# LayerNorm of the attention input applied to transposed tokens, without TensorE transpositions

## The reference

```python
def _layernorm(x, axis=-1, eps=1e-05):
    m = jnp.mean(x, axis=axis, keepdims=True)
    v = jnp.var(x, axis=axis, keepdims=True)
    return (x - m) / jnp.sqrt(v + eps)

# attention: 16 heads of 64, 128 queries and 128 keys in each of 64 sequences
q, k, v = norm_x @ w_q, context @ w_k, context @ w_v
out = softmax(q k^T * 64 ** -0.5) v @ w_o + b_o
# feed-forward: 8 experts of width 512, the best 2 of softmax(x @ gate) weigh their outputs
h = relu(x @ W1[e] + b1[e]);  y = sum over the best 2 of gate_topk[e] * (h @ W2[e] + b2[e])
# block
x = x + attention(_layernorm(x), ctx_768)
x = x + feed_forward(_layernorm(x))
```

## Time and profile before

| what | us |
|---|---|
| median of 3 runs | 1580.39 (1580.01 to 1581.38) |
| profiled execution, its own time | 1580.22 |
| span of the profiled execution | 1578.5 |
| start until the steady iterations | 0 to about 58 |
| one iteration in steady state | 34.16 |
| expert phase | from about 1110 |

### The profile page before, as it was taken

How to read it: one execution, slowest core, us unless ns; L and a number is a source line. 1 busy time by engine, 2 the same in 40 slices (tenths; PEclk the granted TensorE clock), 3 DMA queues, 4 the chain that set the end, 5 groups by cost and what they waited for, 6 DMA issues and landing times.

```text
span 1578.5 us, 45424 instructions
## 1 busy us (share of the span) xinstructions
PE 1553.8 (98%) x14150; PEld 1454.0 (92%) x14151; DVE 1176.1 (75%) x3796; ACT 1108.0 (70%) x3357; POOL 818.1 (52%) x946
## 2 busy tenths in 40 slices
PE   8999999999999999999999999999999999999997
PEld 7899999999899999999999989998899999999997
DVE  4777777777777777777777777777788777777775
ACT  5677677677776777767767777676666676777774
POOL 2344545545554554554555455455456555555556
PEclk9999999999999999999999999999999999999999
DMA  6522111222111221211122211122799755555554
GB/s 201 145 72 74 60 60 60 77 90 72 62 60 60 67 94 66 74 60 60 63 75 89 74 60 60 60 67 81 241 231 249 144 86 85 89 86 90 84 84 61
DMA packets 105643, 145.05 MB, mean 92 GB/s; under 512 B 12736, under 2 KB 87616, under 8 KB 105344
## 3 DMA queue, kind: packets, MB, share of 16 engines
q1 hardware_dynamic: 60144, 89.00, 17.8%
q0 software_dynamic: 26816, 37.32, 13.7%
q10 hardware_dynamic: 18640, 18.19, 4.4%
HBM read 77.09 MB, written 67.38 MB: 92 GB/s over the span
## 4 chain that ended last, share of the span: by engine, by line
issue 47%; POOL 22%; PE 9%; DVE 7%; DMA 6%; DVEq 3%; ACT 2%; POOLq 2%; ACTq 1%; SPq 0%
POOL lists L662 7%; DMA out<-stage_room,number 6%; PE bank_a L1404 4%; POOL prob L669 3%; DVE hid L1332 3%; POOL rstd L648 2%; DVE stage_room L1349 2%; POOL stage_room L711 2%; POOL stage_room L707 2%; POOL out L735 2%; DVEq L1344 1%; PE bank_v L1437 1%; POOLq L729 1%; PE bank_s L1422 1%; DVEq L1323 1%
## 5 line engine op out<-in xcount | busy, mean ns | idle before, releaser
L669 POOL TENSOR_TENSOR prob<-prob,inv 128x512 f32<-128x512 f32 x256 | 271.4, 1060 | 520.3 <-DVE inv L956 519.6
L777 ACT ACTIVATE prob<-bank_s,low 128x128 f32<-128x128 f32 x1024 | 363.3, 376 | 40.9 <-DVE low L951 40.9
L735 POOL DMA_INDIRECT out<-stage_room,number x142 | 231.8, 1632 | 53.9 <-issue 53.1
L951 DVE TENSOR_REDUCE low<-bank_s 128x4 f32<-128x512 f32 x256 | 175.4, 685 | 98.0 <-PE bank_s L1422 97.9
L777 ACT ACTIVATION_READ_ACCUMULATOR prob<-bank_s,low 128x1 f32 x1024 | 221.1, 216 | 0.0
L770 ACT ACTIVATE probt<-bank_t 128x512 f32<-128x512 f32 x256 | 153.4, 599 | 89.6 <-PE bank_t L1411 89.6
L1050 DVE SCALAR_TENSOR_TENSOR stage_room<-xin,wo_t 128x256 f32<-128x256 f32 x480 | 178.8, 426 | 0.0
L807 ACT ACTIVATE ot_h<-bank_v 128x512 fp32r<-128x512 f32 x128 | 77.4, 604 | 138.4 <-PE bank_v L1437 138.4
L885 ACT ACTIVATE hidt_h<-hid 128x512 fp32r<-128x512 f32 x142 | 89.7, 632 | 117.4 <-DVE hid L1332 112.2
L1411 PE MATMUL bank_t<-ident,prob 128*128 128x128 f32 x1024 | 161.9, 281 | 4.0 <-POOL prob L669 4.0
L1404 PE MATMUL bank_a<-xt_l,wq_h 128*128 128x256 f32 x512 | 152.4, 298 | 0.3 <-DVE xt_l L966 0.3
(11 more groups left out here) (231 smaller groups left out, 4728.9 us busy)
## 6 DMA issues: line engine op xcount, KB each, us to landing
stage_room<-lists ACTq DMA_DIRECT2D x67, 265.0 KB
halves<-stage_room SPq DMA_DIRECT2D x32, 512.0 KB
homes<-halves SPq DMA_DIRECT2D x16, 1024.0 KB, 6.4
xin<-in_x SPq DMA_DIRECT2D x32, 256.0 KB, 2.8
stage_room<-in_x SPq DMA_DIRECT2D x32, 256.0 KB
stage_room<-in_w SPq DMA_DIRECT2D x32, 256.0 KB, 4.3
out<-stage_room SPq DMA_DIRECT2D x32, 256.0 KB, 2.2
cin<-in_ctx SPq DMA_DIRECT2D x32, 128.0 KB, 2.6
```

What stands on the lines that cost most here:

```text
L669: pool.tensor_tensor(prob[:, n % 4, :, :], prob[:, n % 4, :, :], wide(inv[:, n % 4, :], P), ALU.mult).then_inc(s_norm.sem, 1)
L735: pool.indirect_dma_start(out, bass.IndirectOffsetOnAxis(ap=number[:, u, b:b + 1], axis=0), ysum[:, u, b, :], None, compute_op=ALU.add).th ...
L777: e = act.activation(prob[:, n % 4, h, :], bank_s[n % 2][:, h * P:(h + 1) * P], ACT.Exp, bias=low[:, n % 4, h:h + 1], scale=-1.0, accum_ou ...
L951: dve.tensor_reduce(low[:, n % 4, :], bank_s[n % 2][:, :].rearrange("p (h k) -> p h k", h=4), AX.X, ALU.min).then_inc(s_low.sem, 1)
```

## The change

- The host also hands over `x_t`, the transposed `x`. SP loads a pair of it into `xraw` (128 x 2 x 2 x 128), between the loads of `xin` and `cin`.
- `t0` and its bank are gone. 15 products are left, with a fixed table of banks (`BANK_OF`).
- Mean and 1/std of each token stand on the partition of the token. To have them along the free axis, SP stores them to DRAM (`ln_rows`, 16 bytes of each partition) and loads the 2 KB back to every partition (`ln_all`, 512 floats in the order token, sequence, statistic). In the first iteration, four PE products with the identity put them into a PSUM bank instead.
- DVE normalises in slot 3, ahead of `o1`'s sum, with two `tensor_tensor` over 128x512 (`normalise_turned`), in place of two `tensor_scalar` over 128x256 in slot 1. The second operand of each reads every fourth float of `ln_all`.
- ACT rounds `xraw` into `xt_h` in slot 4, between `copy_t` and the exponentials; DVE takes the rest (`low_of_tokens`) in slot 4 behind `aggregate`. Both operands of it are now in SBUF.
- The reciprocal of u3 moves from slot 4 (behind `lowest`) to slot 3, ahead of the three `x_scores`; so does the wait for `bn2_1`.

The core of the diff:

```diff
+            def ln_through(sp, it):
+                if not isinstance(it, int) or it > 0:
+                    sp.wait_ge(ln_in, it * 16)
+                wait(sp, pool_step, it, "rstd1")
+                sp.dma_start(ln_rows, mean_var[:, 0, :, :]).then_inc(ln_out, 16)
+                sp.wait_ge(ln_out, it * 16 + 16)
+                wait(sp, xn_step, it - 1, "xn")
+                sp.dma_start(ln_all.rearrange("p t b k -> p (t b k)"), ln_rows.rearrange("t b k -> (t b k)").rearrange(
+                    "(o n) -> o n", o=1).to_broadcast([P, 4 * P])).then_inc(ln_in, 16)
...
                     sp.dma_start(xin[:, :, :], src).then_inc(x_in, 16)
                     cols = bass.ds(row, 2 * P)
+                    sp.dma_start(xraw.rearrange("p c b t -> p c (b t)"),
+                                 x_t[:, cols].rearrange("(c p) t -> p c t", p=P)).then_inc(xt_in, 16)
...
-                        wait(sp, ln1_step, it - 1, "ln1")
+                        wait(sp, xa_lo, it - 1, "x")
+                        wait(sp, ln1_step, it - 1, "bn1_1")
...
                         load_x(it)
+                        ln_through(sp, it)
...
+                        if n == 4 and has(it, NEXT):
+                            wait(act, a_full, it, "q11")
+                            wait(act, xn_step, it, "xn")
+                            act.activation(xt[0][:, 0:DC, :], xraw.rearrange("p c b t -> p c (b t)"),
+                                           ACT.Copy).then_inc(xa_hi.sem, 1)
                         if has(it, CUR):
                             exps(it, n)
...
+                def normalise_turned(it):
+                    dve.wait_ge(xt_in, (it + 2) * 16)
...
+                        dve.wait_ge(ln_in, it * 16 + 16)
+                    dve.tensor_tensor(xraw[:, :, :, :], xraw[:, :, :, :], of_tokens(it, 0), ALU.subtract).then_inc(xn_step.sem, 1)
+                    wait(dve, xn_step, it, "centred")
+                    dve.tensor_tensor(xraw[:, :, :, :], xraw[:, :, :, :], of_tokens(it, 1), ALU.mult).then_inc(xn_step.sem, 1)
+
+                def low_of_tokens(it):
+                    wait(dve, xa_hi, it, "x")
+                    dve.tensor_tensor(xt[1][:, 0:DC, :], xraw.rearrange("p c b t -> p c (b t)"),
+                                      xt[0][:, 0:DC, :].bitcast(F32), ALU.subtract).then_inc(xa_lo.sem, 1)
...
+                        if n not in (0, 4) and has(it, of):
+                            inverse(it, name, n - 1)
+                        if n == 3 and has(it, NEXT) and not (isinstance(it, int) and it < 0):
+                            normalise_turned(it)
...
-                        if n == 1 and has(it, NEXT):
-                            normalise(it, 0, xin, [xn[:, 0, :], xn[:, 1, :]])
...
                             statistics(1, x1)
                             gate_max(it)
+                            after_step(it, "bn2_1")
+                        if n == 3 and has(it, NEAR[4][1]):
+                            inverse(it, NEAR[4][0], 3)
...
-                            for c in range(DC):
-                                last = pe.transpose(dst[:, (2 * c + b) * P:(2 * c + b + 1) * P],
-                                                    xn[:, b, c * P:(c + 1) * P], ident[:, :])
```

More of the change, by code:

```diff
@@ L71, in wait, with program @@
         engine.wait_ge(signal.sem, value - back)
-def program(nc, x, ctx, w_all, w_ot, b_o, b_oc, gate, gate_t, w12, b1, b2, out):
+def program(nc, x, x_t, ctx, w_all, w_ot, b_o, b_oc, gate, gate_t, w12, b1, b2, out):
     tokens, D = x.shape
@@ L108, in program @@
     assert DC * H == HC * D == 2 * QUARTER and E * QUARTERS == PAIRS
+    ln_rows = nc.dram_tensor("ln_rows", (P, 2, 2), F32, kind="Internal").ap()
     A_SLOTS = [
@@ L130, in program @@
         [("o1", FROM0)],
-        [("t0", NEXT), ("v10", CUR), ("v11", CUR)],
+        [("v10", CUR), ("v11", CUR)],
         [],
@@ L138, in program @@
     A_BANKS = 4
-    assert len(A_EVENTS) % A_BANKS == 0
-    HI_EVENTS = [e for e in A_EVENTS if e[0][0] in "tqk"]
+    BANK_OF = {"q10": 0, "k10": 1, "o0": 2, "k11": 3, "q11": 0, "o1": 1, "v10": 2, "v11": 3,
+               "q00": 0, "k00": 1, "q01": 2, "k01": 3, "v00": 1, "f0": 0, "v01": 2}
+    HI_EVENTS = [e for e in A_EVENTS if e[0][0] in "qk"]
     DONE_EVENTS = [e for e in A_EVENTS if e[0][0] not in "qk"]
@@ L359, in by_products, with a_bank @@
                 return isinstance(it, int) and it < 1
[L361 to L367, removed]
+            def a_bank(name):
+                return bank_a[BANK_OF[name]]
             def bank_before(it, name):
+                same = [n for n, _ in A_EVENTS if BANK_OF[n] == BANK_OF[name]]
                 if not isinstance(it, int):
[L372 to L376, removed]
+                    k = same.index(name) - 1
+                    return (it if k >= 0 else it - 1), same[k]
+                order = [(j, n) for j in range(-1, PAIRS + 1) for n in a_full.present(j) if n in same]
+                k = order.index((it, name)) - 1
                 return order[k] if k >= 0 else (it, None)
@@ L647, in rstd_of @@
                     wait(pool, pool_step, it, f"shift{k + 1}")
-                    pool.tensor_tensor(rstd[:, k, :], shifted[:, k, :], mhalf[:, :],
+                    pool.tensor_tensor(mean_var[:, 0, :, 1] if k == 0 else rstd[:, k, :], shifted[:, k, :], mhalf[:, :],
                                        ALU.pow).then_inc(pool_step.sem, 1)
@@ L783, in hi_part @@
                     wait(act, a_full, it, name)
-                    src = a_bank(it, name)
+                    src = a_bank(name)
                     kind, k = name[0], int(name[-1])
-                    if kind == "t":
-                        last = act.activation(xt[0][:, 0:DC, :], src[:, :].rearrange("p (c t) -> p c t", c=DC), ACT.Copy)
-                    elif kind == "q":
+                    if kind == "q":
                         last = act.activation(qt[:, int(name[1]), 2 * k:2 * k + 2, :],
@@ L958, in second_part @@
                 def second_part(it, name):
-                    src = a_bank(it, name)
+                    src = a_bank(name)
                     kind, k = name[0], int(name[-1])
[L961 to L968, removed]
+                    wait(dve, a_full, it, name)
+                    if kind == "v":
                         last = dve.tensor_copy(vv[:, int(name[1]), k, :], src[:, :])
@@ L1035, in rows_of @@
                     dve.wait_ge(sent, (it - 1) * 64 + 16)
-                    normalise(it, 1, x1, [rows[:, b, 0:D] for b in range(2)])
+                    normalise(it, x1, [rows[:, b, 0:D] for b in range(2)])
                 def x_scores(it, first, many):
@@ L1142, in body @@
                             x_scores(it, *X_SCORES[n])
+                        if n == 4 and has(it, NEXT):
+                            low_of_tokens(it)
                         made_in = it - 1 if n == 0 else it
@@ L1365, in _ @@
                 after_step(PAIRS, "bn2_1")
-                aggregate(1)
+                aggregate(PAIRS, 1)
                 x_part(1, 1)
@@ L1448, in product @@
                         wait(pe, a_hi if of[0] in "qk" else a_done, earlier, of)
-                    if kind == "t":
-                        wait(pe, ln1_step, it, "ln1")
-                        for b in range(2):
-                            for c in range(DC):
-                                last = pe.transpose(dst[:, (2 * c + b) * P:(2 * c + b + 1) * P],
-                                                    xn[:, b, c * P:(c + 1) * P], ident[:, :])
-                    elif kind == "q":
+                    if kind == "q":
                         g = int(name[1])
-                        if k == 0:
-                            wait(pe, a_done, it if g == 0 else it - 1, "t0")
+                        if name == "q00":
+                            wait(pe, xa_lo, it, "x")
                         for j in range(2):
@@ L1567, in keep_busy, with first_statistics @@
                                   skip_group_check=True)
+                def first_statistics():
+                    wait(pe, pool_step, -1, "rstd1")
+                    pe.wait_ge(made, 20)
+                    for k in range(2):
+                        for b in range(2):
+                            last = pe.matmul(bank_s[1][:, (2 * k + b) * P:(2 * k + b + 1) * P],
+                                             mean_var[:, 0, b, k:k + 1].to_broadcast([P, P]), ident[:, :],
+                                             start=True, stop=True, skip_group_check=True)
+                    last.then_inc(ln_first, 1)
                 def gate_means():
@@ L1587, in _ @@
                 keep_busy(3)
[L1588 removed]
+                first_statistics()
                 iterations(pe, body)
```

64 lines of the change are left out of this document (39 added, 25 removed).

## The result

The changed kernel takes 1630.49 us (median of 6 runs, 1628.76 to 1636.54), the kernel before in the same comparison 1580.57 (1580.01 to 1581.38): a ratio of 1.0321, 95% interval 1.0305 to 1.0336. That is 50 us slower, and 18 us above the end of the predicted range.

A forecast was written before the change was run, and what follows sets the result against it. PE's instruction order sets the period. A stall of 0.50 to 0.61 less 0.44 gained, times 30, plus 0.6 at the start, on 1580.2 gave 1584 us (likeliest case 1582 to 1586); the range was 1574 to 1612.

The forecast's parts named there:

- The place of the stall: Slot 5: PE's first wk product, k00, waits for DVE's rest of the context, 0.50 to 0.61 us a pair.
- the sum of slot 4: DVE's chain from the tokens' rest (522.03) to the context's end (525.13), against k00 wanted at 524.84: stall 0.34.
- The start behind the release: Slot 5 on PE: k00 starts some 0.05 us behind the end of the context's rest.
- The short power: Slot 4: POOL's two-element power for the second LayerNorm holds DVE's tokens' rest, bounds 0 and 0.27, taken 0.16 to 0.27.
- a normalising step at 0.61: Slot 3 on DVE: each of two normalising steps takes 0.61 us; o1's idle time hides both, with 0.02 lacking.
- the rival with a chance of 0.28: Slot 3: normalising steps slower than 0.61, since they read every fourth float; 1588 to 1612 us, chance 0.28.
- the 0.53: Slot 3: from the first normalising step's start (516.14) until POOL gets the port for norm u2 (516.67).
- from when POOL holds DVE: Slot 3: norm u3 wants the port at 520.20, after the second send (520.17), beside the third x_scores (520.18).
- The rival's own sum: Slots 3 to 5, steps of 1.14: o1's sum 1.07 late, stall 1.47, net 1.03, 1612 us; chance 0.28 for slower steps.
- the length of the sends: Slot 3 on POOL: the second send ends 0.28 later than before, at 520.17, its length taken as before.
- u3's reciprocal as harmless: Slot 3 on DVE: the reciprocal comes 1.8 us earlier, not needed by u3's transpositions, and adds only 0.08.
- the 0.6 for the start: Start of the run: 256 KB of x_t ahead of the weights cost 0.6 us, bounds 0 and 1.3.

The follow-up runs named there:

- e7: e6 with ACT's rounding of the tokens moved to slot 3, behind the exponentials: 1570.74 us, 0.9939 of the kernel before.
- e6: e2 with the three x_scores taken out of slot 3 (8 in slot 1, 6 in slot 2), rounding still in slot 4: 1585.49 us, 1.0026.
- e2: The changed kernel with the statistics laid out so that the normalising steps read every second float (8 bytes): 1603.08 us, 1.0138.
- e1: The changed kernel with means and reciprocals stored apart, so that both normalising steps read densely: 1788.99 us, 1.1317.
- e4: The kernel before with only u3's reciprocal and the wait for bn2_1 moved ahead of slot 3's three x_scores: 1586.14 us, 1.0029.
- e8: e7 with the 16-byte layout of the changed kernel: 1587.15 us, 1.0042.
- e3: The changed kernel with u3's reciprocal back in slot 4, behind the maxima; 16-byte read kept: 1595.67 us, 1.0096.
- e9: e7 with u3's reciprocal put back in slot 4, behind the maxima: 1569.67 us, 0.9939.

## Why the prediction was wrong

**Right: where PE stands and what it gains.** The values would be 0.44 earlier; the iteration's sum closes with it (35.74 against 35.77), and an iteration of e7 is 0.41 shorter than before. The place of the stall, `k00` behind the context's rest, is right too.

**Right: the sum of slot 4.** e6 has its two ends within 0.04 and 0.02. Two small terms were off. The start behind the release is 0.15 and not 0.05, with 0.06 more at the restart. The short power was taken at 0.16 to 0.27 and cost about 0.03 (e6). In the changed kernel this chain isn't what binds, since DVE comes to it 1.54 later (T + 4.53 for T + 2.99).

**Wrong: a normalising step at 0.61.** It takes 1.06 (at most 1.09 for the first one, 31 times). This was the rival with a chance of 0.28, and the sign that the prediction gave for it, a first step of over 0.9, is there. The step that failed is the nearest row: L988 reads 32 elements of PSUM in 0.19, which is what rows 4 lets one expect without any penalty (0.16 for 4 elements, 0.69 for 512), and I let it speak for 512 of SBUF. e2 and e1 show the size in SBUF: 0.66 at 8 bytes, 0.69 densely, and in the changed kernel 1.06 at 16, 1.6 times the 0.66. Why 16 bytes cost and 8 do not, no run shows.

No run shows the 0.53 after which the prediction lets POOL go on beside the first step (516.14 to 516.67). It was my estimate, and the rival's 1.14 is 0.61 and the same 0.53 once more; rows 4 come near it, with 0.69 for 512 elements and 0.16 for 4. The runs show in its place how long norm u2 is held, which takes 1.05 by itself: it lasts 1.30 in e7 (from 511.44, the first step of 0.66 from 511.19) and 1.72 in the changed kernel (from 538.68, the step of 1.06 from 538.43). So, counted back from its end, it went on 0.50 after the start of the step in e7 and 0.92 after it in the changed kernel.

**Wrong: from when POOL holds DVE, and how long its send is.** The rival's own sum, at 1.14 a step, gave a stall of 1.47 and 1612 us; the steps were a little faster than it said, and yet 2.02 were lost. Of the missing 0.55, 0.10 is the release above. The other 0.45 is on POOL: by the rival's sum the rest of the tokens starts at 523.16 - 519.08 = T + 4.08, and measured is T + 4.53. Two steps of the prediction failed there.

The first is the length of the sends, which it took as before. One grew by 0.70 beside the second normalising step, and norm u3 ends at T + 3.20. By the rival's sum it would have ended some 0.5 earlier: norm u2 at 518.25, 2.45 from there to the end of the second send as before (517.43 to 519.88), and 1.05 give 521.75, T + 2.67.

The second is the moment. I let norm u3 hold DVE only from the end of the send before it, so that only an `x_scores` that starts after that is held. If that were so, the late norm would have held none for long: the second `x_scores` starts 0.60 before the norm's recorded start and would have been over in 0.42. It is held to the norm's end; the same in e2 (0.55), e4 (0.06) and e8 (0.17, there the rest of the tokens). In each the reciprocal that releases the norm had been written 0.24 us or more before the held instruction began (542.71 and 542.95 here), and the instruction in front of the second `x_scores`, begun just before the reciprocal was written (542.63 here), ran at 0.39. In e3, where the reciprocal comes later, the same instructions beside the same kind of send run at 0.41 to 0.47. So in these four runs a norm that stood released behind a send held DVE's instruction as if it ran. The release alone is not enough within the first moment: in e9 and e3 the rest of the tokens began 0.05 after it, with POOL idle, and went first. The lengths are measured; why a norm that is not yet recorded holds DVE, no run shows.

The length of 1.96 fits an instruction that stands still for most of it and is not merely slowed: it is the 1.65 until norm u3 ends and 0.31 more, where an `x_scores` alone takes 0.42. A send grows as well: beside the second normalising step it grew from 0.99 to 1.69, and to 1.25 beside the faster one of e7 (at 512.91).

**Wrong: u3's reciprocal as harmless.** I gave it nothing, because u3's transpositions don't need it. What it does is release norm u3 into the `x_scores`. In the kernel before it costs 5 us (e4), in the changed one 35 (e3), and with the `x_scores` moved away nothing (e9). I had noted that the norm comes in then, and let 0.02 us decide who is first.

**Open.** At the start, PE's products of the first 9 us take longer in the profile of the changed kernel than in that of e7 (1.91 against 1.16 for the eight with the identity), at a recorded clock of 1.00 in both, and its first scores come 1.40 later than before, those of e7 only 0.28. The code of the two is the same there, and e2 has the slow start too (0.42 each of the eight, 0.28 in e7), so the layout isn't the cause. What makes the difference I have not found, and the 0.6 for the start is neither confirmed nor refuted.

## What to carry to other kernels

Before an operand is read with a step, look at where it is written: here a layout with 8 bytes from float to float cost DVE nothing (0.66 us, against 0.69 densely), one with 16 took 1.6 times as long (1.06), and the change from one to the other is the order of two dimensions. When a wait of POOL is released earlier, list the two-operand instructions of DVE that then stand beside it, and where the released instruction stands behind a send, count POOL as holding them from the release on: so it was in the changed kernel, where the `x_scores` that began 0.60 before norm u3 took 1.96 for 0.42, and in e2, e4 and e8. And if a removed operation is the gain, its worth is seen only when every chain beside it has that much slack: the rounding in slot 3 was worth nothing until two other edits were made, and then 15 us.

## What the hardware showed unexpectedly

- DVE `tensor_tensor` over 512 floats of 128 partitions, second operand in SBUF: 0.69 us densely (e1), 0.66 with a step of 8 bytes (e2), 1.06 with 16 (the changed kernel).
- A send on POOL (indirect DMA, 0.99) grew to 1.69 beside the second normalising step of the changed kernel, a two-operand instruction of DVE, and to 1.25 beside that of e7.
- A two-operand instruction of DVE that began 0.06 to 0.60 us before the recorded start of a POOL multiply was held to that multiply's end, where the multiply had been released and stood behind a send: an `x_scores` took 1.96 (the changed kernel), 1.90 (e2) and 1.40 (e4) for 0.42, the rest of the tokens 1.78 (e8) for 0.66.
- A store of the same 2 KB: 1.4 us to landing in pieces of 16 bytes (the changed kernel), 3.0 in pieces of 8 (e2), about 8 in pieces of 4 (e1).
